# First attention of a twelve-stage kernel: from spreading the weights over the heads' rows to a band of weights laid out through DRAM

## What is computed

```python
_OFFSETS = list(range(41)) + [128, 48, 192]
q, k, v = jnp.split(x @ w_qkv, 3, axis=-1)      # then 16 heads of 8
idx = jnp.arange(T)[:, None] - deltas[None, :]  # 44 keys for each token
k_mod = k[:, :, maximum(idx, 0)] * (1.0 + scale_embed)
scores = einsum('bhtd,bhtjd->bhtj', q, k_mod) / sqrt(8) + pos_bias
scores = where(idx >= 0, scores, min)
attn = softmax(scores, axis=-1)
out = einsum('bhtj,bhtjd->bhtd', attn, v[:, :, maximum(idx, 0)])
y = (out * if_gain) @ w_out                     # added to x
```

## Time and profile before

| | |
|---|---|
| time, median of 3 runs | 3620.96 us (3615.15 to 3623.59) |
| profiled execution | 3621.11 us, span 3619.3 us |
| TensorE | 3169.1 us busy, 88% |
| VectorE | 2591.5 us, 72% |
| ScalarE | 1834.8 us, 51% |
| GpSimd | 987.1 us, 27% |
| mean granted TensorE clock | 0.926 |
| DMA | 99.76 MB, mean 28 GB/s |

### The profile page before, as it was taken

How to read it: one execution, slowest core, us unless ns; L and a number is a source line. 1 busy time by engine, 2 the same in 40 slices (tenths; PEclk the granted TensorE clock), 3 DMA queues, 4 the chain that set the end, 5 groups by cost and what they waited for, 6 DMA issues and landing times. The chain is left out here.

```text
span 3619.3 us, 60121 instructions
## 1 busy us (share of the span) xinstructions
PE 3169.1 (88%) x23469; PEld 1637.2 (45%) x23509; DVE 2591.5 (72%) x5604; ACT 1834.8 (51%) x3336; POOL 987.1 (27%) x843
## 2 busy tenths in 40 slices
PE   4679876798988999999889998989899799898899
PEld 3212223565652222222256665657677223232677
DVE  8787869887758999999487774463534788884433
ACT  2232222577756777777667773313222257677221
POOL 0345643668630000000196670000300311211100
PEclk9889978899997999999999998989899689999899
DMA  1000000211106000000021110000300500000100
GB/s 51 9 1 1 0 0 12 68 31 36 32 14 211 1 1 1 1 1 1 4 78 29 34 29 29 2 26 1 94 1 1 174 1 30 33 1 1 45 1 12
DMA packets 72849, 99.76 MB, mean 28 GB/s; under 512 B 11748, under 2 KB 51688, under 8 KB 72360
## 3 DMA queue, kind: packets, MB, share of 16 engines
q1 hardware_dynamic: 72568, 95.92, 9.0%
HBM read 62.81 MB, written 19.45 MB: 23 GB/s over the span
## 5 line engine op out<-in xcount | busy, mean ns | idle before, releaser
L1963 ACT ACTIVATE AR<-ps 128x1024 f32<-128x1024 f32 (+2 forms) x756 | 717.8, 995 | 287.3 <-PE ps L1864 218.9
L2046 DVE TENSOR_REDUCE AR<-ps 128x1 f32<-128x512 f32 x1296 | 808.9, 683 | 48.9 <-PE ps L1833 48.2
L1864 PE MATMUL ps<-AR 32*128 32x512 bf16 (+3 forms) x4992 | 532.0, 374 | 10.2 <-ACT AR L1963 6.2
L1833 PE MATMUL ps<-AR 32*128 32x512 bf16 (+3 forms) x1664 | 478.1, 395 | 46.6 <-DVE AR L2046 14.2
L1881 PE MATMUL ps<-AR 128*32 128x512 f32 (+3 forms) x3328 | 435.7, 596 | 4.1 <-ACT AR L1968 3.6
L2614 DVE SCALAR_TENSOR_TENSOR X<-ps,AR,X 128x128 f32<-128x128 f32 x512 | 143.6, 344 | 345.6 <-PE ps L2455 345.3
L2455 PEld LDWEIGHTS ps<-AR 128*128 128x128 f32 x3072 | 362.9, 192 | 60.4 <-issue 47.5
L1833 PEld LDWEIGHTS ps<-AR 32*128 32x128 bf16 x1664 | 119.8, 92 | 551.6 <-DVE AR L2046 412.1
L2455 PE MATMUL ps<-AR 128*128 128x128 f32 x3072 | 363.1, 275 | 0.0
L2430 PE MATMUL ps<-XT,AR 128*128 128x512 f32 x672 | 307.7, 594 | 0.1
L210 POOL TENSOR_TENSOR rs<-rs,halves 128x4 f32<-128x4 f32 x48 | 49.5, 1031 | 822.2 <-DVE rs L202 822.1
(11 more groups left out here) (323 smaller groups left out, 5465.9 us busy)
## 6 DMA issues: line engine op xcount, KB each, us to landing
AR<-AR SPq DMA_DIRECT2D x124, 128.0 KB, 2.3
AR<-in_c_rot SPq DMA_DIRECT2D x64, 128.0 KB, 2.2
AR<-in_L3f_w SPq DMA_DIRECT2D x30, 256.0 KB, 5.4
rows_KA<-AR SPq DMA_DIRECT2D x32, 128.0 KB, 2.4
AR<-scr_bias SPq DMA_DIRECT2D x32, 128.0 KB, 3.2
AR<-in_L2f_w SPq DMA_DIRECT2D x30, 128.0 KB, 2.9
AR<-rows_KC SPq DMA_DIRECT2D x7, 512.0 KB, 6.6
rows_QA<-AR SPq DMA_DIRECT2D x24, 128.0 KB, 2.4
```

What stands on the lines that cost most here:

```text
L1833: e.matmul(g.bank[b][:, 0:w], QA[rows, q, 128 * i:128 * i + 128], KA[rows, q, 512 * first:512 * first + w], start=way != "kept", stop=True ...
L1864: t = e.matmul(g.bank[h][:, lo:512], K[32 * h:32 * h + 32, q, 128 * kt:128 * kt + 128], Q[32 * h:32 * h + 32, q, queries], start=y == 0, s ...
L1963: e.activation(dst[:, :, lo:512], src[:, :, lo:512], ACT.Exp, scale=self.scale).then_inc(*s.up("exp" if u else "left", k, i, *((1,) if u e ...
L2046: e.tensor_reduce(o, g.bank[b][:, 0:w], AXX, ALU.max).then_inc(*s.up("reduced", k, n, h, st, kc))
```

## The change

1. Tokens are reversed. The turn of x is a matmul with the reversing matrix instead of a transpose, Q and K are stored from the last token to the first, K with its 192 zero columns behind (`back`). Scores start as soon as chunk 0 of Q and K is there. Which products GpSimd makes stays as it was, and the gathers too.
2. V is no longer transposed: TensorE computes it with tokens on partitions, one window of 128 tokens at every 64 (`project`, 8 x 4 matmuls), and VectorE copies it to `V` with the gain multiplied in.
3. The layout of softmax is head by distance, so that reductions read neighbouring values; the scores are turned by 12 matmuls with a permuted identity a tile of 128 tokens, over two banks and their neighbours. The steps for tile n stand by themselves in the plan, 0.15 of a chunk apart, instead of four together.
4. Weights: VectorE multiplies the exponentials with the reciprocal straight into `WP`, 112 places a head, of which the 41 neighbours and the one at 48 are filled. SyncE stores `WP` to DRAM with a row pitch of 1800 values and loads it back with a pitch of 1799 (`store`, `load`, two halves of 64 partitions each), by which each token's row is shifted by one more place: 64 tokens share one window of 112 keys. TensorE turns it with the reversing matrix (`turn`, 16 matmuls a tile), ScalarE copies it to `PT`.
5. Values: TensorE multiplies windows of V with the turned band (`value`, 32 matmuls a tile with 112 x 32 weights and 64 columns). The distances 128 and 192 are multiplied by GpSimd (`WF`, `U`, five small products a tile) and added in the same bank by four matmuls. ScalarE copies the bank (`taken`), TensorE projects it with four matmuls (`through`), VectorE adds four tiles to x (`close`).
6. Gone are the bf16 split, `drop`, `spread`, VectorE's 176 value products, GpSimd's 88 pair sums and the final transposes. The first matmul waits for five loads instead of seven; four more bring the output weights later.

The diff, cut to its core:

```diff
-    SCORE_LAG, VALUE_LAG, NPR, NPV = 4, 8, 11, 12
+    SCORE_LAG, NPR, FAR, ROW, KEYS = 4, 11, (41, 43), 1800, 112
...
+        at = []
+        for c in range(4):
+            at += [(c + (i + 0.5) / (2 * NJ), x) for i, x in enumerate(self.scores(c))]
+            at += [(0.1 + 0.1 * b, ("project", 0, 0, b)) for b in range(8) if not c]
+            for i in range(4):
+                soft = c + 1.02 + 0.15 * i
+                at += [(soft, ("lift", c, i, 4 * c + i)), (soft + 0.05, ("exp", c, i, 4 * c + i)),
+                       (soft + 0.12, ("norm", c, i, 4 * c + i))]
+                far = soft + 0.67
+                at += [(far + 0.02 * y, ("turn", c, y, 4 * c + i)) for y in range(4)]
+                at += [(far + 0.1, ("value", c, i, 4 * c + i)), (far + 0.13, ("taken", c, i, 4 * c + i)),
+                       (far + 0.16, ("through", c, i, 4 * c + i))]
+            at += [(far + (0.36 if c == 2 else 0.18), ("close", c, 0, 0))]
...
+        for x in range(14):
+            self.store(e, s, x)
+            if x < 13:
+                self.load(e, s, x)
+        self.load(e, s, 13)
+        self.store(e, s, 14)
+        self.store(e, s, 15)
+        self.load(e, s, 14)
+        self.load(e, s, 15)
+
+    def store(self, e, s, x):
+        k, half = self.k, 64 * self.ROW
+        to = self.g.band[x % 3]
+        e.wait_ge(*s.at("weighted", k, x))
+        if x >= 3:
+            e.wait_ge(*s.at("d_loaded%d" % (4 + x % 3), k, "band", x - 3, 1))
+        for b in range(2):
+            e.dma_start(to[half * b:half * b + half].rearrange("(p n) -> p n", p=64),
+                        self.WP[64 * b:64 * b + 64, x % 2, :]).then_inc(*s.up("d_loaded%d" % (2 * (x % 2) + b), k, "band", x, by=16))
+
+    def load(self, e, s, x):
+        k, n = self.k, 16 * self.KEYS
+        if x >= 3:
+            e.wait_ge(*s.at("p_turned", k, x - 3, 3))
+        for b in range(2):
+            o = 64 * b * self.ROW
+            e.wait_ge(*s.at("d_loaded%d" % (2 * (x % 2) + b), k, "band", x))
+            e.dma_start(self.PB[64 * b:64 * b + 64, x % 3].rearrange("p h m -> p (h m)"),
+                        self.g.band[x % 3][o:o + 64 * (self.ROW - 1)].rearrange("(p n) -> p n", p=64)[:, 0:n]).then_inc(
+                            *s.up("d_loaded%d" % (4 + x % 3), k, "band", x, b, by=16))
...
+            if what == "turn":
+                y = 4 * n + j
+                if j == 0:
+                    e.wait_ge(*s.at("d_loaded%d" % (4 + n % 3), k, "band", n, 1))
+                if y > 1:
+                    e.wait_ge(*s.at("et", k, (y - 2) // 4, (y - 2) % 4))
...
+                for h in range(4):
+                    t = e.matmul(g.bank[4 + y % 2][0:self.KEYS, 128 * h:128 * h + 128], self.PB[:, n % 3, 4 * j + h, :], g.anti,
+                                 start=True, stop=True)
...
+                        for a in range(4):
+                            h = 4 * gr + a
+                            t = e.matmul(g.bank[6][32 * a:32 * a + 32, 128 * gr + 64 * b:128 * gr + 64 * b + 64],
+                                         self.V[0:self.KEYS, o + 8 * h:o + 8 * h + 32],
+                                         self.PT[0:self.KEYS, n % 2, 128 * h + 64 * b:128 * h + 64 * b + 64],
+                                         start=False, stop=gr == 3 and b == 1, skip_group_check=True)
...
+            if what == "norm":
+                e.wait_ge(*s.at("exp", k, n))
+                e.tensor_reduce(self.sm[:, j, :], self.SM[:, j], AXX, ALU.add).then_inc(*s.up("share", k, n, "sum"))
+                e.wait_ge(*s.at("share", k, n, "sum"))
+                e.reciprocal(self.sm[:, j, :], self.sm[:, j, :]).then_inc(*s.up("share", k, n))
...
+                    for b in range(2):
+                        e.wait_ge(*s.at("d_loaded%d" % (2 * (n % 2) + b), k, "band", n - 2))
...
+                e.tensor_tensor(to[:, :, 0:41], self.SM[:, j, :, 0:41], bc(self.sm[:, j, :], [128, 16, 41], 2),
+                                ALU.mult).then_inc(*s.up("weighted", k, n, "run"))
+                e.tensor_tensor(to[:, :, 48], self.SM[:, j, :, 42], self.sm[:, j, :], ALU.mult).then_inc(*s.up("weighted", k, n))
```

More of the change, by code:

```diff
@@ L504, in allocate @@
-        self.S8 = ar.f32(6, 512)
-        self.SM = ar.f32(4, NJ, 16)
+        self.S8 = ar.f32(2, 6, 512)
+        self.SM = ar.f32(4, 16, NJ)
         self.mx = ar.f32(4, 16)
         self.sm = ar.f32(4, 16)
[L508 to L515, removed]
+        self.WP = ar.f32(2, self.ROW)
@@ L517, in scores @@
+        self.plan = [x for _, x in sorted(at, key=lambda y: y[0])]
     def scores(self, c):
@@ L527, in scores @@
         return out
[L529 to L543, removed]
-            if j % 2 and j > self.VALUE_LAG:
-                out.append(("through", c, j - self.VALUE_LAG, 0))
-        return out + [("close", c, 0, 0)]
     def by_pool(self, n):
@@ L627, in tensor @@
[L627 to L638 removed]
+                    m = min(8, NJ - 8 * gr)
@@ new lines, in tensor @@
+            if what == "value":
+                e.wait_ge(*s.at("et", k, n, 3))
+                if n:
+                    e.wait_ge(*s.at("paired", k, n))
+                    e.wait_ge(*s.at("ot", k, n - 1))
+                else:
+                    e.wait_ge(*s.at("v_cleared", k))
+                for gr in range(4):
+                    e.matmul(g.bank[6][:, 128 * gr:128 * gr + 128], self.U[:, n % 2, gr, :], g.anti,
+                             start=gr == 0, stop=False, skip_group_check=True)
+                for gr in range(4):
+                    for b in range(2):
+                        o = 128 * (2 * (15 - n) + 1 - b)
+                        for a in range(4):
+                            h = 4 * gr + a
[3 more added lines that the diff above has]
+                                         start=False, stop=gr == 3 and b == 1, skip_group_check=True)
+                t.then_inc(*s.up("valued", k, n))
@@ L760, in gpsimd @@
-    def gpsimd(self, e, s):
-        g, k = self.g, self.k
-        e.memset(self.W2, 0.0).then_inc(*s.up("taps_cleared", k))
-        e.memset(self.KT[:, 0:PAD], 0.0).then_inc(*s.up("k_padded", k))
-        e.memset(self.VT[:, 0:PAD], 0.0).then_inc(*s.up("v_padded", k))
-        chunks = set()
-        for what, c, j, n in self.plan:
-            if what == "product" and self.by_pool(n):
                 if c not in chunks:
@@ L786, in gpsimd @@
[L786 to L789 removed]
+                elif n >= 7:
+                    e.wait_ge(*s.at("turned", k, 3))
+                o = 512 * (3 - c)
+                e.tensor_tensor(self.PR[n % self.NPR], self.QT[:, o:o + 512], self.KT[:, o + OFFS[j]:o + OFFS[j] + 512],
+                                ALU.mult).then_inc(*s.up("product", k, n))
@@ L2757, in build @@
                   for name in ("KA", "KC", "QA", "QB", "QC")}
+        g.band = [nc.dram_tensor("band%d" % i, (128 * L0Attn.ROW,), F32, kind="Internal").ap() for i in range(3)]
         kinds = [L0Ffn, L0Attn, L0Ffn, L1Ffn, Attn8, L1Ffn, Moe, L2Attn, Moe, Moe, Attn8, Moe]
```

344 lines of the change are left out of this document (167 added, 177 removed).

## The result

| | before | after |
|---|---|---|
| time, median | 3620.57 us (4 runs, 3615.15 to 3623.59) | 3481.93 us (4 runs, 3475.96 to 3482.60) |
| profiled execution, span | 3621.11, 3619.3 us | 3482.60, 3480.8 us |
| the stage | 462.4 us | 320.4 us |
| the rest of the span | 3156.9 us | 3160.4 us |

The account below looks back on a forecast made before the run. TensorE and VectorE, nearly equally full, were taken to bound the 462.4 us stage; 46 + 66 + 158 + 60 = 330 us, 132 less, gave 3489 us. The range was 3430 to 3560, the forecast's own 3465 to 3515.

Parts of the forecast that it names:

- the forecast's case: First attention stage: TensorE leads in chunks 2 and 3, DRAM round trip covered there; 3465 to 3515 us, chance 0.5.
- the trip is covered: Band's store to DRAM and load back cost nothing while chunks follow each other; 12 us uncovered at the stage's end.
- VectorE's work: Score products, GpSimd contention, softmax and residual add on VectorE: 59 us a full chunk, less than TensorE's 68.
- the share of chunks 2 and 3: TensorE busy 0.86 of these chunks, as in the old stage's middle, so 68 us of work takes 79 each.
- the tail: Stage's end after the last gather: last score turn, softmaxes, 12 us store and load, last tile's values; about 60 us.
- start and chunk 0: From the stage's first load through chunk 0: fewer loads and projections first, VectorE also copying V; 46 us.
- TensorE's work: Per full chunk: 43.6 us of float32 matmuls for four tiles plus 24 us of gathers, 68 us.
- The loss beside GpSimd: VectorE's score products lengthened while GpSimd makes its own: 37 us for the stage, 9.3 a chunk.
- Rival 1: Engines hide each other better, chunks at the longer engine's bare sum: stage 294 us, time 3453 us; chance 0.22.
- Rival 3: DRAM round trips of sixteen tiles queue and bound the stage, 39 us a tile: slower, 3840 us; chance 0.04.
- point of decision: Tile period in the DRAM queue, 24.6 us, past which the round trip would make the kernel slower than before.
- signs of being wrong: Load wait ahead of weight turns outside the tail, TensorE waiting for products in chunk 3, or tail beyond 75 us.

Follow-up runs that it names:

- six transposes: Changed kernel with the scores turned by 6 one-pass transposes a tile instead of 12 two-pass matmuls, VectorE reading PSUM at stride 16: 3453.29 us, ratio 0.9538.
- both turns: Kernel with scores turned by 6 transposes a tile, now also turning the weights by one-pass transposes, order restored by ScalarE's backward read: 3434.13 us, ratio 0.9479.

## Why the prediction was right, step by step

The time, 3481.9, is 7 us under the forecast of 3489, and inside its own range of 3465 to 3515. It is the forecast's case that came: TensorE leads in chunks 2 and 3, and the trip is covered. That the number is so near is partly luck. Three terms were wrong by more than the sum shows: VectorE's work, the share of chunks 2 and 3, and the tail. Chunks 2 and 3 took 18 us less than forecast, the tail 8 and the rest of the kernel 3.5 us more, which cancel in part.

The measured borders (161, 225, 297 and 365 us) lie about where TensorE begins to turn the scores of tiles 0, 4, 8 and 12.

| stretch | forecast | measured |
|---|---|---|
| start and chunk 0 | 46 | 48.5 |
| chunk 1 | 66 | 64.0 |
| chunks 2 and 3 | 158 | 140.0 |
| tail | 60 | 68.0 |
| stage | 330 | 320.4 |

**TensorE's work, right in sum.** 68 us a chunk were forecast, and 67.3 were found between the stores of tiles 4 and 8, 64.3 in the next chunk. The gathers took 28 us instead of 24: the count of 20 runs was right, and the price was wrong in both ways. A gather alone takes 1.05 us, not 0.86, and three or four together take no longer; 0.86 a pair rested on the row at the lower clock. A pass of full weights took 70.9/512 = 0.138 us instead of 0.118, so that a tile's turn of weights came to 4.4 us instead of 3.8, and its turn of scores to (41.4 + 10.8)/16 = 3.3 instead of 2.8; against that the band values took 17.6/16 = 1.1 instead of 2.4. Together with far values and projection (1.2 and 1.1) a tile has 11.1 us, and 10.9 were forecast. By these groups a chunk would have about 73 us; the 67.3 are less because groups overlap at their borders, which the sum had not allowed for. A pass of the band values, with 32-column weights, took 0.017 us, under the lower end of 0.02.

**VectorE's work, too high.** 59 us a chunk were forecast, 46.7 found. The loss beside GpSimd was put at 37 us for the stage, from the earlier trace rows of before; it was 116.4 - 144 x 0.683 = 18. Before, the products also ran beside GpSimd's splits and pair sums, which the change removes, and this was overlooked: chunk 0 of before, 28.9 us in all for 36 products, showed less than 4 us of loss in a stretch that had GpSimd's products alone. The trace of before bears it out when each of its 144 products is put down to the GpSimd operation that it overlaps most: beyond 0.683 us each (42 us in all, since the durations of products overlap a little), those beside GpSimd's products lost 16 us, those beside its splits 14 and those beside pair sums 12; the 43 with nothing beside them took 0.682 us. The reductions took 0.88 us and not 1.0: contiguous data was worth the whole of the lower bound. GpSimd's small products cost VectorE nothing that can be seen in the softmax's durations; the score products that ran mainly beside them took 0.90 us instead of 0.68, 4 us in the whole stage, where 3 a chunk were put.

**The share of chunks 2 and 3, too low.** TensorE filled 95% and 94%, not the 86% of the earlier trace rows. That share came from a stretch in which VectorE too had 77 of 100 us, and it was carried over to one in which VectorE has two thirds. The run that filled VectorE to 61 us shows the dependence: chunk 2 took 81.8, at 0.85. With VectorE's work as predicted the prediction's 79 us would nearly have come, so the miss in this term goes with the miss in VectorE's. What carries it is the wait for products behind softmax steps: 3.8 us in the changed kernel's chunk 2, 5.4 and 6.0 in the kernels with less work for TensorE, 12.4 in the one that filled VectorE. How much of the last is the length of the block is not shown. Rival 1 had named the outcome (the engines hide each other better) and gave the finer order of the plan and the single PSUM ring as reasons, which no run tested by themselves; and its chunks at 59 + 68 + 68 = 195 stand against 204 measured.

**The tail, too short, for another reason than its own.** The sum let the last tile wait 12 us for its store and load, and counted TensorE's five tiles as fitting beside it. The timeline shows TensorE's steps for the last tiles one behind the other:

```profile
406.87 2.85 PE L647 MATMUL ps<-C,AR 128*112 128x128 f32 x24
410.41 1.16 PE L658 MATMUL ps<-C,AR 128*128 128x128 f32 x8 [0.69 <-ACT AR L704]
411.50 1.10 PE L665 MATMUL ps<-AR 112*32 112x64 f32 x64
412.53 1.13 PE L647 MATMUL ps<-C,AR 128*112 128x128 f32 x8
413.49 1.06 PE L677 MATMUL ps<-AR 128*128 128x128 f32 x8
414.38 2.85 PE L647 MATMUL ps<-C,AR 128*112 128x128 f32 x24
...
421.90 2.85 PE L647 MATMUL ps<-C,AR 128*112 128x128 f32 x24
```

A tile takes 7.5 us there (406.87, 414.38, 421.90), with nothing but a wait of 0.69 for ScalarE's copy in it, and none waits for its load. The last band is stored at 400.4 and turned at 421.9; without any trip the time was the same, as the run without it showed, and only a second load was too late (7.73 us). Ahead of this queue TensorE waits once for ScalarE, 2.83 us at 398.54: the copy of tile 12's turned weights stands on ScalarE behind the exponentials of the last tiles. What the sum should have had is a queue of tiles on TensorE, and not the way of one tile. The run with closer softmaxes gained nothing that could be measured ahead of that queue; the kernels with fewer passes shortened it, from 58.7 us between the store of tile 12 and the end to 55.8 (six transposes) and 49.9 (both turns).

**The DMA.** 6 us for both halves were taken. A half landed in 4.7 or 5.0 us (medians), both halves of tile 0's store in 5.6 (171.10 to 176.7) and both of its load in 6.3 (175.13 to 181.4), the whole trip in 10.3 where 12 stood in the sum. SyncE's period of 6 us, one store, was right; the stores are farther apart because VectorE gives them so. Rival 3's price of 39 us a tile was wrong, its mechanism was right (518 by its formula, 517.18 measured, with the luck told above), and its point of decision, 24.6 us, was that for slower than before; the point from which the gain shrinks is estimated at 15.1 us, and SyncE's own period stands 9 us below it. The Trainium skill (SBUF — State Buffer, "Can I just issue two DMAs to hit both halves?") says that two transfers to the two halves serialise; no run here has one half alone to compare with. The prediction's estimate from that page, 6.5 us each way, is near the 5.6 and 6.3 measured; the trip is shorter than twice 6.5 since each half is loaded as soon as it is stored.

**What was to show it.** Found as named: no value product on VectorE, TensorE over 85% busy at a granted clock of 0.98 and 1.00 in chunks 2 and 3, a load that no weight turn waits for, a tail under 75 us. Not as named: the score products, 116.4 us instead of unchanged at 135; the band's passes; the turns' passes, 0.138 us and not 0.12; and SyncE, which waits 190.9 us for VectorE, as said, but 53.4 for its own stores too. One of the signs of being wrong came, in small: TensorE waited for products in chunk 3, 4.2 us in five waits. It belonged to the forecast's case all the same, since a share of 0.86 allowed for more idle time than that.

**The start.** 48.5 instead of 46: TensorE (38.2 of 39.3 us) was fuller than VectorE (35.3) in chunk 0, with 23.0 us of gathers, 9.4 of V's projections (7.6 forecast) and what was left of Q's and K's.

Open is the 3.5 us outside the stage, and how the longer waits for products in the run that filled VectorE divide between the sum of its work and the length of its blocks.

## What to carry to other kernels

The share that the leading engine reaches goes with the work of the second one: 0.95 with the second's work at 0.7 of the leader's, 0.85 to 0.90 at about 0.9 of it, in nearly the same plan. Look for the waits behind the difference: here they are waits for products that stand in the second engine's queue behind longer steps. A loss by contention measured before has to be divided by whom it was lost to, and goes with that work. Before a duration is taken from a row, look at the granted clock of its stretch: the price of the gathers came from one at 0.50. When a step's chain at the end of a stage is priced, price the queue of the busiest engine there first; and in a stage that TensorE bounds, look for float32 matmuls that only permute: a transpose is one pass, and the permutation can go into the read of PSUM, worth 48 us here.

## What the hardware showed that was not expected

- A pass with 112 x 32 float32 weights on 64 columns took 17.6/1024 = 0.017 us, four heads of which write different rows; one with 64-column weights took 0.038.
- VectorE's read of PSUM with a step of 16 values took 0.89 us for 704 values, as long as the contiguous one; a reduction in SBUF over a step of 16 took 1.34 and over neighbours 0.88.
- ScalarE's copy out of PSUM that reads backwards took 594 ns for 512 values, forwards 596.
- 32 products moved from GpSimd to VectorE left VectorE's busy time as it was, 115.6 against 116.4 us.
